# Ranks of routed nodes from one scan and one product; routing and experts in one block

## The reference, cut to what matters

```python
rh = relu(features @ router_w1 + router_b1)
probs = softmax(rh @ router_w2 + router_b2)
top_w, top_i = top_k(probs, 2)
weights = softmax(top_w)
h1 = relu(features @ w1[e] + b1[e])
h2 = relu(h1 @ w2[e] + b2[e])
expert_out = h2 @ w3[e] + b3[e]
combined = sum over the two chosen e of expert_out * weight
x = x + combined
```

## Time and profile before

| | |
|---|---|
| median of 3 runs | 2250.74 us (2250.05 to 2253.19) |
| the profiled execution's own time | 2249.98 us |
| its span on the core | 2248.2 us |
| mean granted TensorE clock | 0.914 of full speed |
| busy: TensorE / VectorE / ScalarE / GpSimd | 83% / 74% / 64% / 53% of the span |

### The profile page before, as it was taken

The page is one execution under the profiler, slowest core; times in us unless marked ns, Lnnn a source line. Parts: engine busy times, 40 slices in busy tenths (PEclk is TensorE's granted clock), DMA queues, the critical chain, the costliest instruction groups (busy, mean ns, idle before and its releaser), DMA issues. The chain is left out here.

```text
span 2248.2 us, 49591 instructions
## 1 busy us (share of the span) xinstructions
PE 1867.2 (83%) x10102; PEld 1504.5 (67%) x10102; DVE 1667.0 (74%) x5284; ACT 1443.1 (64%) x4425; POOL 1199.3 (53%) x1169
## 2 busy tenths in 40 slices
PE   3788857699945999999999999999997671799996
PEld 2445435477734778778788787787786561688885
DVE  7888888877654888888888898988887642355553
ACT  5666568144303889889898898898987650333332
POOL 2010000056565777777777777777771377255554
PEclk9999978599756999999999999999999675899998
DMA  4321111021103444444444444444441543355553
GB/s 144 92 77 57 51 28 51 19 86 46 38 22 89 123 118 117 122 120 119 119 118 118 118 115 122 118 118 121 116 118 33 196 160 131 66 93 93 93 96 53
DMA packets 133895, 215.45 MB, mean 96 GB/s; under 512 B 42813, under 2 KB 89084, under 8 KB 133604
## 3 DMA queue, kind: packets, MB, share of 16 engines
q0 software_dynamic: 61920, 132.16, 24.4%
q1 hardware_dynamic: 67022, 72.68, 11.0%
q10 hardware_dynamic: 4662, 7.46, 1.1%
HBM read 150.28 MB, written 56.51 MB: 92 GB/s over the span
## 5 line engine op out<-in xcount | busy, mean ns | idle before, releaser
L1389 POOL DMA_INDIRECT area<-wh_table,area x788 | 769.2, 976 | 257.6 <-issue 235.3
L1716 PE MATMUL bank<-area 128*126 x1960 | 483.1, 389 | 27.9 <-ACT area L1636 14.7
L1716 PEld LDWEIGHTS bank<-area 128*126 128x126 f32 x1960 | 348.9, 188 | 100.7 <-issue 51.8
L1422 DVE TENSOR_SCALAR area<-iota_row,area 128x126 f32<-128x126 f32 x980 | 355.7, 370 | 25.8 <-ACT area L1589 17.4
L1622 ACT ACTIVATE area<-iota_row,area 128x126 f32<-128x126 f32 x735 | 285.9, 389 | 0.0
L2207 POOL DMA_INDIRECT out_dram<-area x108 | 169.4, 1569 | 163.5 <-DVE area L2268 146.8
L1636 ACT ACTIVATE area<-area 128x126 f32<-128x126 f32 x735 | 237.0, 386 | 0.4
L585 POOL DMA_INDIRECT sorted_slots<-area x112 | 134.9, 1204 | 118.9 <-DVE area L941 90.0
L1575 ACT ACTIVATE area<-bank 125x512 bf16<-125x512 f32 x245 | 145.5, 594 | 76.5 <-DVE area L1436 73.7
L1736 PE MATMUL bank<-area 128*128 128x250 f32 x800 | 188.4, 378 | 6.6 <-ACT area L1643 3.5
L1747 PE MATMUL bank<-area 128*125 128x256 f32 x800 | 188.9, 379 | 0.0
(11 more groups left out here) (410 smaller groups left out, 4049.6 us busy)
## 6 DMA issues: line engine op xcount, KB each, us to landing
area<-moe_rows SPq DMA_DIRECT2D x54, 264.0 KB, 2.8
area<-wh_table,area POOLq DMA_INDIRECT x788
area<-area SPq DMA_DIRECT2D x17, 388.5 KB
wh_table<-area SPq DMA_DIRECT2D x50, 126.5 KB
xn<-in_x_dram SPq DMA_DIRECT2D x25, 250.0 KB
xt_rows<-area SPq DMA_DIRECT2D x50, 125.0 KB, 2.5
area<-xt_rows SPq DMA_DIRECT2D x25, 250.0 KB
x_rows<-area SPq DMA_DIRECT2D x25, 250.0 KB
```

What stands on the lines that cost most here:

```text
L1389: g.indirect_dma_start(out=gath[:, (i + GT) % RS, :], out_offset=None, in_=table, in_offset=bass.IndirectOffsetOnAxis(ap=idx_tab[:, i:i + ...
L1422: ins = V.tensor_scalar(xm[:, b, t, :], iota_row[:, :], rowl[:, j % 10, t:t + 1], fetched(j, D)[:, t:t + 1], ALU.is_equal, ALU.mult)
L1716: last = T.matmul(bank[US[b]][0:RW, 0:WROW], sm[:, b, t, :], gath[:, bass.ds(place + t, 1), 0:WROW].rearrange("p a w -> p (a w)"), start=( ...
```

## The change

1. `ranks`: the products for single tiles are gone. VectorE makes one running sum over a group's tiles (`tensor_tensor_scan`, restarted for each expert by a 0 in `going`), takes `sel` away from it, and TensorE adds the result with one product for the group. `sel` now stands as expert by tile.
2. The features and shares are written in place into `pay`, the array of the attention sums (its rows are 264 wide now), instead of `pay3`; `posi` holds the positions of all 50 tiles. GpSimd's copies of ids are gone.
3. Routing and experts are one block. After the third group a first count is taken. `table_of(0)` makes the table's first 20 entries (`FULL`) from it: only tiles of 256 rows that the first 26 node tiles fill for sure. `table_of(1)` makes the other 34 from the full counts. So the order of the row tiles becomes: for each expert its tiles full after 26 node tiles, then for each expert the further full ones, then one remainder tile for each.
4. SyncE gathers tiles 0 to 19 once the first three groups' rows have landed and the first table is there, and before tile 20 writes the blanks and waits for all rows. The ring has four tiles instead of six; the weights and ids are copied out of it (`share`, `node`).
5. GpSimd writes three tiles of the last group, and the other nine one by one behind the adds of expert tiles 0 to 8.

```diff
-RB6 = 6
-assert MT % PB3 == 0 and sum(SIZES) == NT and max(SIZES) == ST and len(SIZES) == NS
+OFF = 4 * 2 * NT
+RING3 = 4
+EARLY = 3
...
-                sp.wait_ge(counted, 1)
                 ends = [sp.alloc_register(f"end{i}") for i in range(2)]
-                for e in range(NX):
-                    sp.reg_load(ends[e % 2], blank_i[0:1, e:e + 1])
-                    b = sp.snap(ends[e % 2], min_val=0, max_val=(NX - 1) * REG + N)
-                    sp.dma_start(moe_rows[bass.ds(b, MR), :].rearrange("(p s) c -> p s c", s=2), pair).then_inc(blanked, 16)
-                sp.wait_ge(blanked, 16 * (NX + 1))
-                sp.wait_ge(base_out, 16 * NS)
-                sp.wait_ge(wx_in, 16 * len(loadsx))
+                regs = [sp.alloc_register(f"base{i}") for i in range(2)]
+                for b in range(PB3):
+                    sp.wait_ge(sent[b], sent_rows[b])
+                sp.wait_ge(tabled, 1)
+                for j in range(MT):
+                    if j == FULL:
+                        sp.wait_ge(tabled, 2)
+                        for e in range(NX):
+                            sp.reg_load(ends[e % 2], blank_i[0:1, e:e + 1])
+                            b = sp.snap(ends[e % 2], min_val=0, max_val=(NX - 1) * REG + N)
+                            sp.dma_start(moe_rows[bass.ds(b, MR), :].rearrange("(p s) c -> p s c", s=2), pair).then_inc(blanked, 16)
+                        sp.wait_ge(blanked, 16 * (NX + 1))
+                        sp.wait_ge(sent_late, 16 * 2 * sum(SIZES[EARLY:]))
+                    sp.reg_load(regs[j % 2], base_i[0:1, j:j + 1])
+                    b = sp.snap(regs[j % 2], min_val=0, max_val=NX * REG)
+                    if j >= 3:
+                        sp.wait_ge(t_t, j - 2)
+                    if j >= RING3:
+                        sp.wait_ge(d_wb, 2 * (j - RING3 + 1))
...
+                def write(g, i, signal):
+                    for k in range(2):
+                        t = first_tile(g) + i
+                        g_.indirect_dma_start(out=moe_rows, out_offset=bass.IndirectOffsetOnAxis(ap=posi[:, k, t:t + 1], axis=0),
+                                              in_=pay[:, t, :], in_offset=None).then_inc(signal, 16)
+
+                def ready_to_write(g):
+                    g_.wait_ge(a_feat, first_tile(g + 1))
                     g_.wait_ge(d_cw, g + 1)
                     g_.wait_ge(d_pos, g + 1)
-                    for i in range(n):
-                        for k in range(2):
-                            g_.indirect_dma_start(out=moe_rows, out_offset=bass.IndirectOffsetOnAxis(ap=posi3[:, b, k, i:i + 1], axis=0),
-                                                  in_=pay3[:, b, i, :], in_offset=None).then_inc(sent[b], 16)
-                for g in range(NS - PB3, NS):
-                    g_.wait_ge(sent[g % PB3], 16 * 2 * (turns_of(g) + SIZES[g]))
+
+                for g in range(NS - 1):
+                    ready_to_write(g)
+                    for i in range(SIZES[g]):
+                        write(g, i, sent[g] if g < EARLY else sent_late)
+                g = NS - 1
+                ready_to_write(g)
+                for i in range(AHEAD_OF_ADDS):
+                    write(g, i, sent_late)
+                g_.wait_ge(base_out, 16 * NS)
+                for j in range(MT):
+                    g_.wait_ge(d_y, 2 * j + 2)
+                    for s in range(2):
+                        g_.indirect_dma_start(out=out, out_offset=bass.IndirectOffsetOnAxis(ap=node[:, j % RING3, s:s + 1], axis=0),
+                                              in_=yo[:, j % 3, s, :], in_offset=None, bounds_check=last_node, oob_is_err=False,
+                                              compute_op=ALU.add).then_inc(sent[j % PB3], 16)
+                    if AHEAD_OF_ADDS + j < SIZES[g]:
+                        write(g, AHEAD_OF_ADDS + j, sent_late)
+                for j in range(MT - PB3, MT):
+                    g_.wait_ge(sent[j % PB3], landed(j))
...
+                def table_of(k):
+                    lo, hi, n = ((0, FULL, NX), (FULL, MT, SEG))[k]
+                    count = bank[CN][:, NX * k:NX * (k + 1)]
+                    whole = fulls[:, NX * (k + 1):NX * (k + 2)]
+                    cmp = cmp_mem[:, 0:(hi - lo) * n].rearrange("p (j s) -> p j s", s=n)
+                    shape = [128, hi - lo, n]
+                    step_n = seg_step.rearrange("p k e -> p (k e)")[:, 0:n]
...
+                    if k == 1:
+                        V.tensor_tensor(blank_i, count, reg6, ALU.add)
+                    step(V.tensor_copy(count_i, count))
+                    step(V.tensor_scalar(count_i, count_i, MR_BITS, None, ALU.logical_shift_right))
+                    step(V.tensor_copy(whole, count_i))
+                    if k == 1:
+                        step(V.scalar_tensor_tensor(odd6, whole, -float(MR), count, ALU.mult, ALU.add))
+                        step(V.scalar_tensor_tensor(fulls[:, SEG:SEG + NX], odd6, 1.0, whole, ALU.min, ALU.add))
+                    V.tensor_tensor(seg_off[:, 0:n], fulls[:, 1:1 + n], fulls[:, NX:NX + n], ALU.subtract)
+                    step(V.tensor_tensor(seg_n[:, 0:n], fulls[:, NX:NX + n], fulls[:, 0:n], ALU.subtract))
+                    V.scalar_tensor_tensor(seg_off[:, 0:n], seg_off[:, 0:n], float(MR), step_n, ALU.mult, ALU.add)
+                    step(V.tensor_tensor_scan(seg_end[:, 0:n], ones[:, 0:n], seg_n[:, 0:n], 0.0, ALU.mult, ALU.add))
+                    step(V.tensor_tensor(cmp, iota_j[:, lo:hi].unsqueeze(2).to_broadcast(shape), seg_end[:, 0:n].unsqueeze(1).to_broadcast(shape), ALU.is_ge))
+                    step(V.tensor_tensor(cmp, cmp, seg_off[:, 0:n].unsqueeze(1).to_broadcast(shape), ALU.mult))
+                    step(V.tensor_reduce(both_f[:, lo:hi], cmp, AX.X, ALU.add))
+                    step(V.scalar_tensor_tensor(both_i[:, lo:hi], iota_j[:, lo:hi], float(MR), both_f[:, lo:hi], ALU.mult, ALU.add))
+                    V.tensor_scalar(base_i[:, lo:hi], both_i[:, lo:hi], PACK - 1, None, ALU.bitwise_and)
+                    step(V.tensor_scalar(ej_i[:, lo:hi], both_i[:, lo:hi], PACK_BITS, None, ALU.logical_shift_right))
+                    step(V.tensor_copy(ej_f[:, lo:hi], ej_i[:, lo:hi]))
+                    for back, clear in ((1, clear1), (2, clear2)):
+                        a = max(lo, back)
+                        step(V.tensor_tensor(change[:, back - 1, a:hi], ej_f[:, a:hi], ej_f[:, a - back:hi - back], ALU.not_equal))
+                        step(V.scalar_tensor_tensor(clear[:, a:hi], change[:, back - 1, a:hi], 32.0, gone[:, a - back:hi - back], ALU.mult, ALU.add))
+                    V.tensor_scalar(base_i[:, lo:hi], base_i[:, lo:hi], float(NX * REG), None, ALU.min).then_inc(tabled, 1)
+
                 def route(g):
-                    b, n = g % PB3, SIZES[g]
+                    n, f = SIZES[g], first_tile(g)
...
-                    V.tensor_tensor(cum[0:R, g + 1, :], cum[0:R, g, :], csum[0:R, :], ALU.add).then_inc(d_cum, 1)
+                    turned_sel = sel[0:R, :, 0:n].rearrange("p e t -> p t e")
+                    V.tensor_tensor(turned_sel, oh1[0:R, 0:n], oh2[0:R, 0:n], ALU.add).then_inc(d_sel, 1)
+                    dve.wait_ge(d_sel, 2 * g + 1)
+                    step(V.tensor_tensor_scan(seen_mem[0:R, :], going_mem[0:R, :], sel_mem[0:R, :], 0.0, ALU.mult, ALU.add))
+                    V.tensor_tensor(iw[0:R, 0:n], seen[0:R, :, 0:n].rearrange("p e t -> p t e"), turned_sel, ALU.subtract).then_inc(d_sel, 1)
+                    V.tensor_tensor(cum[0:R, g + 1, :], cum[0:R, g, :], seen[0:R, :, ST - 1], ALU.add).then_inc(d_cum, 1)
                     dve.wait_ge(a_ee, g + 1)
                     step(V.tensor_scalar(dn[0:R, 0:n], ee[0:R, 0:n], 1.0, None, ALU.add))
                     step(V.reciprocal(w_a[0:R, 0:n], dn[0:R, 0:n]))
...
+                    if g == EARLY:
+                        table_of(0)
...
-                    T.matmul(bank[PB][0:R, 0:n * NX], tri3[0:R, 0:R], sel[0:R, 0:n].rearrange("p t e -> p (t e)"), start=True, stop=False)
-                    for i in range(n - 1):
-                        T.matmul(bank[PB][0:R, (i + 1) * NX:n * NX], ones[0:R, 0:R],
-                                 sel[0:R, i, :].unsqueeze(1).to_broadcast([R, n - 1 - i, NX]), start=False, stop=False, skip_group_check=True)
-                    T.matmul(bank[PB][0:R, 0:n * NX], ones[0:R, 0:R], cum[0:R, g, :].unsqueeze(1).to_broadcast([R, n, NX]),
-                             start=False, stop=True).then_inc(t_rank, 1)
...
+                    V.tensor_copy(share[:, j % RING3, :, :], rowt[:, j % RING3, :, D:D + NX])
+                    step(V.tensor_copy(node[:, j % RING3, :], rowi[:, j % RING3, :, MW - 2]))
...
+                    else:
+                        dve.wait_ge(wx_in, 16 * len(loadsx))
+                        stage1(0)
+                        stage1(1)
+                        stage2(0)
+                    route(g)
...
+                    if j == 1:
```

(20 more changed lines are left out.)

419 lines of the change are left out of this document (184 added, 235 removed).

## The result

The changed kernel takes 2224.22 us (median of 4 runs, 2220.27 to 2229.12), the kernel before 2251.97 beside it (4 runs, 2250.05 to 2253.91): a ratio of 0.9878, 95% interval 0.985 to 0.9906. The forecast was 2213, with a range of 2197 to 2234. The gain is 27.8 us where 37.6 were summed, so the direction held and the time lies in the range, but outside the likeliest case of the prediction (2205 to 2219).

The account below looks back on a forecast made before the run. Experts were taken as bound by TensorE, so the weight lay on how early their loop starts. Terms -57.2 + 4.0 + 4.0 + 1.5 + 1.2 + 8.9 = -37.6 us gave 2213, range 2197 to 2234.

Parts of the forecast that it names:

- the likeliest case: The forecast as summed, with the time within 2205 to 2219 us; chance 0.50.
- The start: Expert loop starts before all rows are written: tile 0's output at 1881.7 instead of 1938.88, 57.2 us gained.
- (a): Second table on VectorE after tile 1's turn takes 6.6 us and makes tile 4's copy late: 4.0 us lost.
- changes 1 and 2: Changes of expert at tiles 1 and 2, whose waits for adds were to hide behind the second table.
- (b): GpSimd's adds and writes take 6.3 us a tile against 5.62; at tile 8's expert change TensorE stalls 4.0.
- (c): Six blanks in SyncE's queue before tile 20: 13.1 us after gather 19's issue, 11.6 free, so 1.5 lost.
- (d): Expert changes at tiles 24, 25 and 26 in a row: 3.7 us late, a stall of 1.2.
- (e): The end: every tile from 47 changes expert; outputs 46 to 53 take 46.8 us instead of 37.9, 8.9 lost.
- The clock's fall: Rival: TensorE's clock falls in waits (a), (b), (d); two cold products each, 3.6 us per wait: 2224; chance 0.17.
- Slow writes beside VectorE: Rival: GpSimd's writes cost 0.5 us more each beside the experts, 7.4 for 14, paid at tile 8: 2220; chance 0.11.
- The ring of four: Rival: gathers landing later than some 6.4 us delay every tile; no faster from 7.1, 2275 at 7.6; chance 0.03.
- the late start: Rival: gather 0 lands only after all writes, so the loop starts as before: 2260; chance 0.02.

Follow-up runs that it names:

- the table in parts: Changed kernel with VectorE's second table cut into four parts behind the turns of tiles 1 to 4, instead of all behind tile 1: 2217.13 us.
- the repeat: The changed kernel measured once more without any edit, for the spread of its executions: 2221.27 us (2220.09 to 2223.42).
- the order's run: Changed kernel with each expert's remainder tile right behind its own full tiles, not at the end of all: 2209.87 us.
- four edits: Changed kernel with blanks one by one before gathers 8 to 13, remainders behind their expert, writes spread and second table in four parts: 2208.62 us.
- fewer writes: Changed kernel with one row write behind each add of tiles 0 to 7 and two behind tiles 8 to 12, none left out: 2221.16 us.

## Why the prediction was nearly right

**The start, -57.2, measured -59.0.** The mechanism held: first gather at 1842.39, no wait for it, the fall of the clock in the wait for ranks (tile 1's product took 3.37), three rank products in place of thirteen. The 1.8 us more come from three places. Tile 0's transpose and product were not cold: 0.63 and 1.97, where I had 1.12 and 3.75, so from the transpose to the exponential of group 4 it took 4.2 us and not 6.6. Against that the router of group 4 ended at 1854.12, 1.2 later than I had it (the stage began 2.2 earlier in this run): ScalarE no longer waited at the row that I named, but 1.72 us at the next. The exponential:

```profile
1858.17 0.26 ACT L2276 ACTIVATE own_mem<-own_mem 125x72 f32<-125x72 f32 x1
```

The remaining 0.6 is the way from tile 1's product to output 0, 12.65 us where I had 13.2.

**(a), 4.0, measured 6.1.** The table took 6.0 us (1879.95 to 1885.98, with its wide instructions at 0.80 as taken) and TensorE idled 3.92, as I had it. Two things were wrong. I wrote that changes 1 and 2 hide behind the table; the runs show that table and changes hide each other. With the table in parts that idle was gone (waits of 0.5 to 2.1 us in its place), and output 8 came no earlier. So the size is right, but the term is not what the table costs. And the products behind the wait were slow: 2.58 and 3.05 for 1.90, 1.8 us more.

**(b), 4.0, measured 5.9.** The lag was sized well: I had output 8 come 6.5 late, it came 6.5 after its turn (12.13 less 5.64), and TensorE idled 4.16 where I had 4.0. The turn was 6.45 for 6.3. Again the product after the wait was missing from the term: 3.46 for 1.90.

**(c), 1.5, measured 6.7: the step that failed.** I counted 13.1 us from gather 19 to gather 20's landing (my three terms, 7.21, 3 and 3.1, make 13.3) and 11.6 free. It was 14.7 (1973.13 to 1987.86): 0.8 to the first blank, 7.3 for the six, 3.2 until they had landed and 3.4 for the gather. And the free time was 9.8, since TensorE was ready at 1982.92: tile 14, where the expert changes, had held back the release of gather 19, which waits for tile 15's turn on VectorE (until 1972.58). So 4.94 of idle, 0.5 for a slow transpose and 1.0 for a slow product; in the repeat the idle was 5.78. I had laid two events side by side that lie one behind the other. The run with the blanks moved confirms the place and the size (6.9). Two of the recorded signs failed here: no idle between tiles 9 and 19, and a clock of 1.00 after 1890 (0.89 in the windows of 1930 and 1980).

**(d), 1.2, measured 3.5.** Tiles 24 to 26 cost 2.4 by output 29 (36.12 from output 23, for six tiles at 5.622), and each lone change leaves a few tenths instead of none. The pace itself is 5.64 for 5.622, which is 0.5 over 26 tiles.

**(e), 8.9, measured 9.8**, and the order's run gives 8.4 of it back.

**The rivals.** The clock's fall was the case in part, and is most of what (a) and (b) lacked. In the windows above the granted clock is 0.92 over the end of the idle at 1934 to 1936.5 and 0.50 just behind it, which is 1.2 GHz. Behind the 3.92 us at the table it was still 1.00 to the end of the idle and fell while TensorE was working again: 0.78 over the first product, 0.60 over the second. After the three waits of 3.9 to 4.9 us one or two products ran slow, at 1.5 to 1.8 us a wait, about half of the 3.6 that the rival had. That its 2224 is the measured time is chance: (c) made up the rest. The Trainium skill (TensorE: Matmul & The Clock Gate, "HAM oscillation — how this bites in real kernels") has gaps in a loop re-throttle TensorE again and again; the trace agrees for the waits of 3.9 us and more. The case of that section is one of long waits; what short ones cost here is in the rows of 2180.45 to 2200.85: behind 1.05 and 1.34 us of idle the product took 2.00, behind 3.05 it took 2.43, behind 4.31 it took 3.78.

*Slow writes beside VectorE* were not the case: between the adds 16 of the 18 writes took 0.98 to 1.04, the other two 1.18 and 1.22, so under 1 us in all, where the rival had 7 (0.5 each). *The ring of four* and *the late start* were not either: the gathers' median to landing is 2.9, and only gather 20 was late, behind the blanks. That no experiment changed the clock without changing a wait stays open: its share is read from rows, not shown by a run.

## What to carry to other kernels

Work that starts earlier keeps its gain only as far as the queues in the middle have room: of 59 us won at the start 31.5 went back, at places where an in-order queue (SyncE's blanks, GpSimd's writes between adds, the last chain of changed tiles) met a wait for landed adds. Sum such terms along the chain, with the lateness of one put into the free time of the next, and add the slow product that follows each wait of TensorE. Before counting on an early start, list what stands ahead of the first output in each queue: here four gathers, not one.

## What the hardware showed that I had not expected

A product of eight records took 1.90 us in the loop. Behind waits it was mostly longer the longer the wait, but not in step with it: 2.00 after 1.05 and (with four edits) after 2.51, 2.43 after 3.05, 3.46 after 4.16 but also (with the table in parts) after 2.50, 3.60 (in the repeat) after 3.48, and 3.78, twice the 1.90, after 4.31 and (with fewer writes) 5.28. After 3.92 two products shared it, with 2.58 and 3.05. So the length of the last wait alone does not give the price. And an indirect write costs GpSimd nearly the same whether VectorE works or not: 0.97 in VectorE's 5.83 us of idle ahead of output 0, mostly 0.98 to 1.04 in the loop.
